# One-hot tensors with pairs of tokens innermost, the score bias added on TensorE, numbers at ranks picked in bf16, and longer loop bodies

## What is computed

```python
q = (x @ Wq + bq).reshape(-1, 8, 128)              # 8 heads
q1, q2 = q[..., :64], q[..., 64:]
s1 = einsum('bhc,hnc->bhn', q1, keys[:, 0])         # 64 keys per side
s2 = einsum('bhc,hnc->bhn', q2, keys[:, 1])
s1t, i1 = top_k(s1, 8)
s2t, i2 = top_k(s2, 8)
all_scores = s1t[..., :, None] + s2t[..., None, :]  # 8 x 8 pairs
all_idx = i1[..., :, None] * 64 + i2[..., None, :]
scores, best = top_k(all_scores, 8)
indices = take_along_axis(all_idx, best)            # rows of two tables of 4096 x 128
inner = einsum('bd,bhkd->bhk', x, w_down[indices])
vals = relu(inner) * softmax(scores)
out = einsum('bhk,bhkd->bd', vals, w_up[indices])
```

## Time and profile before

| | us |
|---|---|
| three runs: median (lowest to highest) | 10608.58 (10585.94 to 10624.52) |
| the profiled execution | 10547.1 |
| its span on the core | 10545.3 |
| PE busy, of the span | 8543.6 (81%) |
| DVE busy | 7228.1 (69%) |
| ACT busy | 3185.1 (30%) |
| POOL busy | 1881.5 (18%) |

### The profile page before, as it was taken

How to read it: one execution, slowest core, us unless ns; L and a number is a source line. 1 busy time by engine, 2 the same in 40 slices (tenths; PEclk the granted TensorE clock), 3 DMA queues, 4 the chain that set the end, 5 groups by cost and what they waited for, 6 DMA issues and landing times. The chain is left out here.

```text
span 10545.3 us, 229521 instructions
## 1 busy us (share of the span) xinstructions
PE 8543.6 (81%) x81842; PEld 6522.5 (62%) x81842; DVE 7228.1 (69%) x25836; ACT 3185.1 (30%) x6691; POOL 1881.5 (18%) x2393
## 2 busy tenths in 40 slices
PE   7777767776777767776377777769999999999999
PEld 7555545554555545554255555558888888888888
DVE  2555545555555545555899999968888888888887
ACT  0333333333333333333244444421111111111111
POOL 0111111111111111111344444410000000000000
PEclk8777777776777767777688888878888888888888
DMA  6322332233223223332000000000000000000000
GB/s 162 38 36 31 38 41 35 31 38 41 33 34 38 35 36 37 38 38 29 3 5 4 5 5 4 4 27 8 8 8 7 8 8 7 8 8 8 7 8 7
DMA packets 349824, 254.32 MB, mean 24 GB/s; under 512 B 38023, under 2 KB 347562, under 8 KB 348493
## 3 DMA queue, kind: packets, MB, share of 16 engines
q1 hardware_dynamic: 348876, 242.70, 15.9%
HBM read 61.50 MB, written 13.04 MB: 7 GB/s over the span
## 5 line engine op out<-in xcount | busy, mean ns | idle before, releaser
L617 DVE TENSOR_REDUCE negmax<-PAIR 99x4 f32<-99x788 f32 x1088 | 1063.9, 978 | 1176.1 <-PE PAIR L373 1037.1
L1399 PEld LDWEIGHTS f_AA<-f_hotp,f_hot 64*128 64x128 bf16 x38400 | 1388.2, 158 | 121.8 <-issue 102.6
L1399 PE MATMUL f_AA<-f_hotp,f_hot 64*128 64x32 bf16 x38400 | 1440.2, 254 | 11.4 <-DVE f_hot L1625 6.9
L373 PE MATMUL PAIR<-ks,qs 96*99 96x198 bf16 x4352 | 809.8, 327 | 675.0 <-DVE negmax L617 570.8
L373 PEld LDWEIGHTS PAIR<-ks,qs 96*99 96x99 bf16 x4352 | 536.8, 166 | 1102.1 <-DVE negmax L617 868.5
L528 ACT ACTIVATE probs<-PAIR 99x792 f32<-99x792 f32 x1024 | 850.3, 830 | 999.8 <-PE PAIR L383 999.1
L1457 ACT ACTIVATE f_act<-f_IN 128x512 f32<-128x512 f32 x800 | 482.2, 603 | 1679.0 <-PE f_IN L1387 1678.8
L1387 PE MATMUL f_IN<-f_zT,f_wd 128*128 128x256 f32 x3200 | 984.0, 469 | 0.0
L1387 PEld LDWEIGHTS f_IN<-f_zT,f_wd 128*128 128x128 f32 x3200 | 760.4, 244 | 291.3 <-issue 138.9
L383 PE MATMUL PAIR<-qs,ks 99*99 99x198 bf16 x4096 | 745.0, 322 | 129.9 <-ACT probs L528 112.9
L1635 DVE TENSOR_TENSOR f_act<-f_act,f_AA 128x512 f32<-128x512 f32 x800 | 510.8, 680 | 483.9 <-PE f_AA L1399 483.8
(11 more groups left out here) (174 smaller groups left out, 13624.0 us busy)
## 6 DMA issues: line engine op xcount, KB each, us to landing
qs<-parts SPq DMA_DIRECT2D x816, 99.0 KB, 4.3
ks<-parts SPq DMA_DIRECT2D x816, 99.0 KB, 5.4
xbuf<-x_in SPq DMA_DIRECT2D x64, 588.0 KB, 4.4
f_hx<-tokens SPq DMA_DIRECT2D x50, 128.0 KB, 2.5
f_hr<-tokens SPq DMA_DIRECT2D x50, 128.0 KB, 2.3
out<-f_hr SPq DMA_DIRECT2D x50, 128.0 KB, 1.8
qs<-mrows SPq DMA_DIRECT2D x272, 9.3 KB
tokens<-h SPq DMA_DIRECT2D x64, 49.5 KB
```

The lines of the kernel that those rows point to most:

```text
L373: mm = nc.tensor.matmul(ps[:, hh, qc * W:qc * W + W], qs[0:STACK, par, 2 * p + hh, j, qc * C:qc * C + C], ks[0:STACK, par, 2 * p + hh, j, ...
L617: V.tensor_reduce(negmax[:, j, :, 2 * p:2 * p + 2].rearrange("p q h -> p h q"), ps[:, :, 0:2 * W].rearrange("p h (q k) -> p h q k", q=2)[: ...
L1399: mm = nc.tensor.matmul(AA[slot][c][:, t * NP:t * NP + NP], hot[64 * c:64 * c + 64, g % 2, :, tt], hotp[64 * c:64 * c + 64, g % 2, pt, :, tt],
```

## The change

Five things at once:
- The loop body of attention holds 8 images instead of 2, that of the FFN 4 steps instead of 2 (`UNROLL`, `TURN`), with 6 steps written out.
- `f_hot`, `f_hotp`, `f_hotc`, `f_iota` and `f_part` are laid out with pairs of tokens innermost (`TL` = 2): neighbouring columns of one token are 2 bf16 apart. The number of elements per instruction stays.
- The bias is split once into three bf16 parts on three partitions, and a second matmul of 512 columns adds it in PSUM, with a column of ones. ScalarE copies the scores out, in its queue between its `relu`s, and waits once a step for `cols_done` of the step itself.
- The rank comparison is one bf16 instruction of 2048 elements against a constant `f_places8`, the product with the numbers a second, and `add_up` three sums of 1024, 512 and 256 elements.
- `f_topf` and `f_rankf` are bf16 with heads innermost, so their casts write or read with strides; `places` and `split_cols` do the same work in the new order.

```diff
-        steps = lambda eng: eng.Fori(0, B // 2)
+        UNROLL = 8
+        steps = lambda eng: eng.Fori(0, B // UNROLL)
...
-                for par in range(2):
-                    n = it * 2 + par
+                for k in range(UNROLL):
+                    n, par = it * UNROLL + k, k % 2
...
+TL = 2
+TURN = 4
...
+INNER = (0, 2, 5, 8, 10, 13, 16)
...
-        bc = sb("f_bc", [TP, 2 * HEADS * FK])
-        iota = sb("f_iota", [128, 128, TG], BF16)
+        bias = sb("f_bias", [3, 2 * HEADS * FK], BF16)
+        ones = sb("f_ones", [3, TP], BF16)
+        iota = sb("f_iota", [128, 128, TL], BF16)
...
-        topf = sb("f_topf", [TP, SEG, 2, TK])
+        topf = sb("f_topf", [TP, TK, 2, 2, HEADS], BF16)
...
-        rankf = sb("f_rankf", [TP, 2, SEG, TK])
-        got = sb("f_got", [TP, 2, SEG, TK])
+        rankf = sb("f_rankf", [TP, 2, 2, TK, HEADS], BF16)
+        places8 = sb("f_places8", [TP, TK, 2 * R], BF16)
+        same = sb("f_same", [TP, TK, 2 * R], BF16)
+        pick = sb("f_pick", [TP, TK, 2 * R], BF16)
+        half = sb("f_half", [TP, TK // 2 + TK // 4, 2 * R], BF16)
+        got = sb("f_got", [TP, 2, R])
...
-        part = sb("f_part", [128, 2, 3, TP], BF16)
+        part = sb("f_part", [128, 2, TP // TL, 3, TL], BF16)
...
-        hotc = sb("f_hotc", [128, 1, NP, TG], BF16)
+        hotc = sb("f_hotc", [128, 1, TG // TL, NP, TL], BF16)
...
-            if NS > 4:
-                with eng.Fori(1, NS // 2 - 1) as it:
-                    for par in range(2):
-                        yield it * 2 + par, it, par, True, True, True
-            for n in range(max(NS - 2, 2), NS):
+            turns = max((NS - 4) // TURN, 0)
+            if turns:
+                with eng.Fori(0, turns) as it:
+                    for k in range(TURN):
+                        yield it * TURN + (k + 2), it * (TURN // 2) + (1 + k // 2), k % 2, True, True, True
+            for n in range(2 + turns * TURN, NS):
...
+                sp.wait_ge(split, 5)
+                for k in range(3):
+                    sp.dma_start(bias[k:k + 1, :], bparts[0:1, k, :]).then_inc(bias_loaded, 16)
+                sp.wait_ge(bias_loaded, 48)
...
+                nc.vector.tensor_copy(bparts[:, 0], bc[:]).then_inc(split, 1)
...
+
+        hot = sb("f_hot", [128, 2, TG // TL, 128, TL], BF16)
         act_in = sb("f_act", [128, 2, NP, STEP])
-        hotp = sb("f_hotp", [128, 2, 3, NP, TG], BF16)
+        hotp = sb("f_hotp", [128, 2, TG // TL, 3, NP, TL], BF16)
...
-                nc.tensor.matmul(WK[:], zT[:, par, c * TP:c * TP + TP], wc[:, 512 * f:512 * f + 512],
-                                 start=True, stop=True).then_inc(s_ready.sem, 1)
+                nc.tensor.matmul(WK[:], zT[:, par, c * TP:c * TP + TP], wc[:, 512 * f:512 * f + 512], start=True, stop=False)
+                nc.tensor.matmul(WK[:], ones[:], bias[:, 512 * f:512 * f + 512], start=False, stop=True).then_inc(s_ready.sem, 1)
...
-                            mm = nc.tensor.matmul(AA[slot][c][:, t * NP:t * NP + NP], hot[64 * c:64 * c + 64, g % 2, :, tt],
-                                                  hotp[64 * c:64 * c + 64, g % 2, pt, :, tt],
+                            mm = nc.tensor.matmul(AA[slot][c][:, t * NP:t * NP + NP], hot[64 * c:64 * c + 64, g % 2, tt // TL, :, tt % TL],
+                                                  hotp[64 * c:64 * c + 64, g % 2, tt // TL, pt, :, tt % TL],
...
+            def copy_scores(fr, par, k):
+                c, f = k // 2, k % 2
+                upto(act, s_ready, fr, k + 1)
+                nc.scalar.copy(sc[:, par, c, 4 * f:4 * f + 4].rearrange("p h s k -> p (h s k)"), WK[:]).then_inc(s_taken.sem, 1)
...
-                if has1:
-                    if behind:
-                        upto(act, out_ready, n - 1, 1)
-                        act.sem_inc(spare, 1)
-                    relu(n + 1, 1 - par, range(0, 12))
-                    exps(n + 1)
-                    relu(n + 1, 1 - par, range(12, NP // 2))
+                    upto(act, cols_done, n, 1)
+                    act.sem_inc(spare, 1)
+                if has1 and behind:
+                    upto(act, out_ready, n - 1, 1)
+                    act.sem_inc(spare, 1)
+                for u in range(2, UNITS):
+                    if has2 and 3 <= u < 7:
+                        copy_scores(n + 2, par, u - 3)
+                    if has1:
+                        relu(n + 1, 1 - par, range(INNER[u - 2], INNER[u - 1]))
+                        if u == 5:
+                            exps(n + 1)
 
...
-                V.tensor_copy(topf[:], topi[:])
+                V.tensor_copy(topf[:].rearrange("p a d c h -> p (c h) d a"), topi[:])
...
-                mark(V.tensor_copy(rankf[:], rank[:]))
-
-            def pick_of(par):
-                return sc[:, par].rearrange("p c h s k -> p (c h s k)").rearrange("p (d s k a) -> p d s k a", d=2, s=SEG, k=TK)
-
-            def numbers_at_ranks(fr, par):
-
+                for d in range(2):
+                    last = V.tensor_copy(rankf[:, d].rearrange("p c k h -> p c h k"), rank[:, d].rearrange("p (c h) k -> p c h k", c=2))
+                mark(last)
+
+            def numbers_at_ranks(fr):
                 met(fr)
-                pick = pick_of(par)
-                for side in range(2):
-                    for a in range(TK):
-                        last = V.scalar_tensor_tensor(pick[:, side, :, :, a], rankf[:, side], float(a),
-                                                      topf[:, :, side, a:a + 1].to_broadcast([TP, SEG, TK]),
-                                                      ALU.is_equal, ALU.mult)
-                mark(last)
-
-            def add_up(fr, par):
+                mark(V.tensor_tensor(same[:],
+                                     rankf[:].rearrange("p d c k h -> p (d c k h)").rearrange("p (o r) -> p o r", o=1
+                                                                                             ).to_broadcast([TP, TK, 2 * R]),
+                                     places8[:], ALU.is_equal))
                 met(fr)
-                mark(V.tensor_reduce(got[:].rearrange("p d s k -> p (d s k)"), pick_of(par).rearrange("p d s k a -> p (d s k) a"),
-                                     axis=AX.X, op=ALU.add))
+                mark(V.tensor_tensor(pick[:].rearrange("p a (e k h) -> p (a e) k h", k=TK, h=HEADS),
+                                     same[:].rearrange("p a (e k h) -> p (a e) k h", k=TK, h=HEADS),
+                                     topf[:].rearrange("p a d c h -> p (a d c) h").rearrange("p e (o h) -> p e o h", o=1
+                                                                                            ).to_broadcast([TP, 4 * TK, TK, HEADS]),
+                                     ALU.mult))
+
+            def add_up(fr):
+                met(fr)
+                mark(V.tensor_tensor(half[:, 0:4], pick[:, 0:4], pick[:, 4:8], ALU.add))
+                met(fr)
+                mark(V.tensor_tensor(half[:, 4:6], half[:, 0:2], half[:, 2:4], ALU.add))
+                met(fr)
+                mark(V.tensor_tensor(got[:].rearrange("p d r -> p (d r)"), half[:, 4], half[:, 5], ALU.add))
 
...
+            def spread(x, k):
+                return x.rearrange("p (a o l) -> p a o l", o=1, l=TL).to_broadcast([128, TG // TL, k, TL])
 
             def hot_group(n, par, g):
                 t0 = g * TG
                 upto(dve, hotp_done, n, g)
-                V.tensor_tensor(hotc[:, 0], idx[:, par, 1:2, t0:t0 + TG].to_broadcast([128, NP, TG]), iota[:, 0:NP, :],
+                V.tensor_tensor(hotc[:, 0], spread(idx[:, par, 1, t0:t0 + TG], NP),
+                                iota[:, 0:NP, :].rearrange("p (o n) l -> p o n l", o=1).to_broadcast([128, TG // TL, NP, TL]),
                                 ALU.is_equal).then_inc(hotc_done.sem, 1)
                 if g >= 2:
                     upto(dve, aa_ready[1], n, g - 1)
...
                     upto(dve, aa_ready[1], n - 1, g + 3)
                 dve.sem_inc(spare, 1)
                 upto(dve, hotc_done, n, g + 1)
-                V.tensor_tensor(hotp[:, g % 2], hotc[:].to_broadcast([128, 3, NP, TG]),
-                                part[:, par, :, t0:t0 + TG].rearrange("p (k o) t -> p k o t", o=1).to_broadcast([128, 3, NP, TG]),
+                e = 3 * t0 // TL
+                V.tensor_tensor(hotp[:, g % 2], hotc[:].rearrange("p o a n l -> p a o n l").to_broadcast([128, TG // TL, 3, NP, TL]),
+                                part[:, par].rearrange("p a k l -> p (a k) l")[:, e:e + 3 * TG // TL].rearrange(
+                                    "p (e o) l -> p e o l", o=1).to_broadcast([128, 3 * TG // TL, NP, TL]).rearrange(
+                                        "p (a k) n l -> p a k n l", k=3),
                                 ALU.mult).then_inc(hotp_done.sem, 1)
-                V.tensor_tensor(hot[:, g % 2], idx[:, par, 0:1, t0:t0 + TG].to_broadcast([128, 128, TG]), iota[:],
```

(2 more changed lines are left out.)

91 lines of the change are left out of this document (48 added, 43 removed).

## The result

The changed kernel takes 9801.59 us in the median of four runs (9766.43 to 9821.72), the kernel before beside it 10597.26 (10564.24 to 10624.52): a ratio of 0.9247, interval 0.9208 to 0.9286. The gain is 796 us, where I had forecast 10,130 and a range from 9,940: right in sign, wrong in size. The profiled execution's span is 9799.0 us, against 10545.3.

The account below looks back on a forecast made before the run. It took DVE to bound attention and PE the FFN. From the profiled 10547.1 us, attention -89, FFN -395 and preparation +8 gave 10071; with 61 added, 10,130 us. Range: 9,940 to 10,530, the forecast's own 10,020 to 10,270.

Parts of the forecast that it names:

- Attention, -89: Attention's loop: 8 images per body turn 32 loop ends into 8, each saving 3.7 us of DVE, 89 us in all.
- Rival D: Attention: unrolling pays nothing because the pause comes with the number of instructions; kernel at 10,220 us, chance 0.03.
- f_AA, -5.3 us per step: FFN on PE: dense reads bring a load and matmul pair from 35.7 to 28.8 ns, saving 5.3 us per step.
- PE still bounds, with 2 us to spare: FFN step after the change: DVE is ready at 56.8 us, before PE ends the second unit at 58.5.
- Rival C: FFN: f_AA pairs take 25 ns, so DVE bounds at about 58.5 us per step; kernel at 9,950 us, chance 0.12.
- DVE's side: FFN on DVE: one-hot writes cost the same, copies leave and picks shrink; work per step falls from 57.7 to 53.8 us.
- B: FFN: the innermost pair costs DVE its whole bf16 pace, 16.8 us per step; slower kernel, 10,707 us, chance 0.05.
- B': FFN: the innermost pair costs DVE two thirds of that loss, 11.2 us per step; kernel at 10,430 us, chance 0.03.
- Bias matmuls +0.9: FFN on PE: four added matmuls of 512 bf16 columns cost 0.9 us per step, 1.8 at the lower clock.
- The loop end, -0.6: FFN on PE: with 4 steps per body the loop-end pause falls from 1.2 to about 0.6 us per step.
- Preparation, +8: Setup, once: five operations, nine memsets and three small DMAs, less a smaller f_iota, add 8 us (2 to 14).
- +61, the median above the profiled execution: Whole kernel: the earlier runs' median, 10608.6 us, lay 61 above the profiled execution, so 61 was added to the forecast.

Follow-up runs that it names:

- hot2_hotp32: The changed kernel with 32 tokens innermost again in the streamed f_hotp, while the loaded f_hot keeps pairs; 10,202 us.
- tl1: The changed kernel with one token innermost in the one-hot tensors, so columns of a token lie 2 bytes apart; 10,630 us.
- tl32: The changed kernel with 32 tokens innermost again in the one-hot tensors, columns 64 bytes apart as before; 10,648 us, ratio 1.0035.

## Why the prediction was right or wrong

*Attention, -89.* Right, and the mechanism too: -90.6 in the spans, -78 alone, and the adds into h lie 25.3 us apart but for every eighth, at 29.0 to 29.8. Rival D fell.

*f_AA, -5.3 us per step: the step that failed.* It measured 8 x (3.57 - 1.30) = -18. That windows at clock 1.00 and 0.50 hold equally many instructions had told me that reads set the pace, and this holds. The error was to take the fastest pace seen in the old layout, 28.8, for the one without conflict. It is the pace of the streamed operand alone at 64 bytes: hot2_hotp32 runs at 28.8 in the median unit at full clock, and at 28.2 to 29.2 in all of them, although its loaded columns lie near. My reading now is that the staggered unit of the earlier trace rows had hidden the loads and kept the stride; no run shows what the stagger changes. And the bound of 25 ns was half a step beyond what was seen, with no reason that excluded more: the range failed there.

*"PE still bounds, with 2 us to spare".* Wrong by that term alone. Rival C's mechanism came in: PE at 49 us, DVE sets the step. My walk along DVE had it at 56.8 us at the end of a step, and 56.5 were measured in the steps without a loop end. C gave 9,950 for 9,802: 1.9 us of step for pauses too many (95 us), and the 61 us below.

*DVE's side.* 53.8 us forecast, with 0.4 of waits in it, and 53.0 measured. f_hot, f_hotc and f_hotp kept their times; B and B' fell. That the repeated single word keeps the pace, read from f_pairs, was right; tl1 shows that half a word loses it. The Trainium skill (Vector Engine (DVE) Microarchitecture Reference, Measured stream behaviour on trn2) asks for runs of two adjacent words; with 2285 ns for 4096 elements nothing of that is seen here. The scores' copies on ScalarE take 586 ns (603 forecast), and DVE doesn't wait for them. The picks with their casts saved more than forecast: counted without overlaps they take 4.5 us a step for 6.9 before, -2.4 for -1.5. The casts' lengths grew from 2 x 0.29 us to 738 and 2 x 538 ns, but the next operation starts before they end, and counted so they cost 0.2 us more a step (0.3 forecast).

*PE's other terms.* Bias matmuls +0.9: 0.31 us from start to start each at full clock (8237.23 to 8237.54), 1.2 per step. In the PE-bound tl32, leaving them out and giving the copies back to DVE took 3.4 off the step, part of it with a higher clock whose cause isn't settled. The wait of the turned columns, +0.5: 2.8 us (135.2 in 48), since PE came earlier. The clock, 3.1 us: it no longer matters, as PE has 7.5 us to spare. One run tests these terms together: hot2_hotp32 has units at the pace that I forecast and PE busy for 63.6 of 64.3 us. Its step is 64.3 for 62.1 forecast, and the kernel 10,202 for 10,130. So with the forecast's own pace the rest of PE's sum was 2.2 us too low; which term, that run doesn't split. The loop end, -0.6 at a PE-bound step: now 3 us in every fourth step, through DVE's wait for PE's chain.

*Preparation, +8.* tl32 has 202.1 us between the last add into h and the first into f_hr, the kernel before 200.5: about 2.

*+61, the median above the profiled execution.* The changed kernel's median lies within 3 us of its profiled span; the offset belonged to one execution of before. Of the 328 us between forecast and result it makes 61, and the step 5.5 x 50 = 275; attention and preparation, 2 and 6 us too dear, add up with them to 344, and the tower's 12 us later start of attention goes the other way.

## What to carry to other kernels

When a run of many small matmuls costs the same at both clock levels, look at how far apart in memory its columns lie, for the loaded and the streamed operand separately, and don't take the best pace of the old layout for the floor of the new one; try the next layout's size on the engine that writes it as well (here 4 bytes for both, 2 is worse for VectorE). A large gain on the bounding engine makes the next engine's work worth what it wasn't: reckon the second bound with its fixed order, and reckon edits together, since the same ones cost 3 us a step on one side of the crossing and gained 5.7 on the other. Where two engines hand over once per step, put independent work into the wait ahead of the handover, not behind it. What an edit takes off an engine is read from starts, not from lengths: the casts' 1.8 us of lengths were 0.8.
